# A twelve-sublayer network on one core: norm moments computed in the sublayer before, weight sums moved, and a skip term added in PSUM by a diagonal matrix

## The reference, cut to what matters

```python
def _layernorm(x, axis=-1, eps=1e-05):
    m = jnp.mean(x, axis=axis, keepdims=True)
    v = jnp.var(x, axis=axis, keepdims=True)
    return (x - m) / jnp.sqrt(v + eps)

x = x + sublayer(_layernorm(x, axis=-1), ...)       # twelve times, with twelve sublayers
```

```python
_, ys = jax.lax.scan(step, state0, xs)
y = jnp.moveaxis(ys, 0, -1)
y = y + D[None, :, None] * u
y = y * jax.nn.silu(z)
```

## Time and profile before

| | |
|---|---|
| runs | 2441.73, 2445.35, 2446.42 us, median 2445.35 |
| profiled execution | 2442.86 us |
| its span | 2441.0 us |
| mean granted clock of PE | 0.864 of full speed |
| norm blocks of stages 4, 6, 7, 8, 9, 10, 11 | one each |

### The profile page before, as it was taken

How to read it: one execution, slowest core, us unless ns; L and a number is a source line. 1 busy time by engine, 2 the same in 40 slices (tenths; PEclk the granted TensorE clock), 3 DMA queues, 4 the chain that set the end, 5 groups by cost and what they waited for, 6 DMA issues and landing times. The chain is left out here.

```text
span 2441.0 us, 34752 instructions
## 1 busy us (share of the span) xinstructions
PE 1988.1 (81%) x11321; PEld 1310.9 (54%) x11337; DVE 1754.3 (72%) x3900; ACT 1345.1 (55%) x2646; POOL 420.7 (17%) x585
## 2 busy tenths in 40 slices
PE   6999999987666666766877895597999999958978
PEld 4776767764333333543654353455766676733545
DVE  6878888777999998647785874674736373568734
ACT  5777777766989896254334365423323333352641
POOL 2333333322111110003532000201101010110000
PEclk8999999997877777786787798598999999976989
DMA  5000000002111102304202100150000000042010
GB/s 222 3 2 2 3 3 2 1 1 99 58 59 59 40 1 66 114 9 86 54 2 75 51 3 18 49 201 2 1 2 0 2 0 2 1 115 70 16 37 18
DMA packets 62030, 94.52 MB, mean 39 GB/s; under 512 B 9403, under 2 KB 48139, under 8 KB 59415
## 3 DMA queue, kind: packets, MB, share of 16 engines
q1 hardware_dynamic: 58604, 87.81, 11.4%
q0 software_dynamic: 1728, 4.22, 0.8%
q10 hardware_dynamic: 1536, 0.49, 0.1%
HBM read 80.53 MB, written 10.49 MB: 37 GB/s over the span
## 5 line engine op out<-in xcount | busy, mean ns | idle before, releaser
L1260 DVE SCALAR_TENSOR_TENSOR moe_acc<-moee_eo,moe_wsel,moe_acc 128x256 f32<-128x256 bf16 x512 | 226.0, 512 | 0.6
L867 DVE SCALAR_TENSOR_TENSOR l_acc<-l_px,l0w_chan,l_acc 128x253 f32<-128x253 f32 (+2 forms) x288 | 137.6, 478 | 80.6 <-POOL l_acc L835 80.1
L1192 ACT CAST moee_eo<-moee_po 128x512 bf16<-128x512 f32 x256 | 132.5, 596 | 38.5 <-PE moee_po L1165 33.8
L1165 PE MATMUL moee_po<-moee_db,moee_hb 96*128 96x256 bf16 (+1 forms) x768 | 126.9, 329 | 26.1 <-ACT moee_eo L1192 15.5
L1150 PE MATMUL moee_pu<-moe_xb,moee_wb 128*128 128x512 bf16 x192 | 73.1, 522 | 83.4 <-DVE moee_ub L1249 83.4
L1165 PEld LDWEIGHTS moee_po<-moee_db,moee_hb 96*128 96x128 bf16 (+1 forms) x768 | 87.6, 116 | 73.0 <-ACT moee_eo L1192 20.9
L1704 ACT ACTIVATE l3xa_ex<-l3xa_pS 128x512 f32<-128x512 f32 x128 | 74.2, 606 | 81.1 <-PE l3xa_pS L1617 76.7
L1704 ACT ACTIVATE l2a_ex<-l2a_pS 128x512 f32<-128x512 f32 x128 | 73.8, 606 | 76.7 <-PE l2a_pS L1617 72.2
L540 PE MATMUL l_pz<-xT,l0w_w_in 128*128 128x256 f32 x384 | 111.4, 414 | 2.5 <-DVE l_sz L915 2.5
L351 PE MATMUL ln_pt<-ident,xn 128*128 128x128 f32 x176 | 39.6, 418 | 85.9 <-DVE xn L277 85.9
L540 PE MATMUL l_px<-xT,l0w_w_in 128*128 128x256 f32 x384 | 103.5, 394 | 4.3 <-DVE l_acc L867 4.3
(11 more groups left out here) (614 smaller groups left out, 5508.3 us busy)
## 6 DMA issues: line engine op xcount, KB each, us to landing
moe_wf<-in_moe_up SPq DMA_DIRECT2D x48, 256.0 KB, 2.8
l3w_w_in<-in_l_w_in SPq DMA_DIRECT2D x1, 8224.0 KB, 25.9
m1b_bc<-bc_rows SPq DMA_DIRECT2D x16, 512.0 KB, 10.4
moe_df<-in_moe_down SPq DMA_DIRECT2D x48, 128.0 KB, 3.2
l_qs<-parts_q SPq DMA_DIRECT2D x36, 128.0 KB
l0w_w_in<-in_l_w_in SPq DMA_DIRECT2D x2, 1536.0 KB, 12.7
l0w_w_out<-in_l_w_out SPq DMA_DIRECT2D x1, 3072.0 KB
parts_q<-l_pieces SPq DMA_DIRECT2D x16, 192.0 KB, 2.3
```

The costliest lines, as they stand in the source:

```text
L867: nc.vector.scalar_tensor_tensor(out=a, in0=px[:, 0:S - (L0_CONV - 1 - c)], scalar=w, in1=a, op0=ALU.mult, op1=ALU.add).then_inc(tap_done, 1)
L1165: last = nc.tensor.matmul(po[:, t, :], hb[rows, j % H, t * P:(t + 1) * P], db[rows, j % H, :], start=(n == 0), stop=(n == len(parts) - 1))
L1192: nc.scalar.copy(eo[:, e % 2, 2 * q:2 * q + 2, :], po[:, 2 * q:2 * q + 2, :]).then_inc(o_read, 1)
L1260: last = nc.vector.scalar_tensor_tensor(out=acc[:, t, :], in0=eo[:, e % 2, t, :], scalar=wsel[:, t, e:e + 1], in1=acc[:, t, :], op0=ALU.mu ...
```

## The change

1. `moments_ahead` computes moments (bn_stats, one `link`, bn_aggr) in the block before the norm, into buffers that now live for the whole kernel. `normalize` gets `ahead`, the number of tiles whose moments are there: 6 in stages 4, 6, 7, 9, 10 and 11, 4 in stage 8. It then begins with `guess(0)`. Stages 0, 1, 2, 3 and 5 stay.
2. The calls stand in attend behind residual(0), (1) and (2); in ternary, a tile at a time; in quant_experts ahead of `unscale(7)`; in half_tokens, a tile at a time; in the l3e block ahead of the wait for the projection.
3. ACT's table for Ln and Exp is loaded at the end of attend, ternary and half_tokens instead of at the start of the norm.
4. `scale_and_sum`: units 0 to 7 stand one at each tile of half_tokens, units 8 to 15 in the l3s block, behind the decay rows. The matmuls of L3166 move behind the token projections and wait for the last unit.
5. The ones in rowsL and rowsR are written by POOL in the half_tokens block.
6. m1b: POOL makes two diagonal matrices of D in m1a. PE adds them times u into py, two matmuls a batch, where DVE's L2149 is removed; the gate multiplication reads py. The first of the two waits for `y_done` of the batch before.

```diff
+def moments_ahead(nc, g, link, tiles):
+    for t in tiles:
+        last = nc.vector.bn_stats(g["stats"][:, t, :], g["res"][:, t, :])
+    link(last)
+    for t in tiles:
+        nc.vector.bn_aggr(g["mv"][:, t, :], g["stats"][:, t, :])
...
+                if ahead:
+                    guess(0)
+                    for t in range(ahead, NT):
+                        stat(t)
+                    newton_a(0)
+                    for t in range(ahead, NT - 1):
+                        aggregate(t)
+                    newton_b(0)
+                    aggregate(NT - 1)
...
                 newton_c(0)
                 guess(1)
                 shifts(0)
...
-                nc.scalar.preload_act_table_set(EXP_LN)
+                if not ahead:
+                    nc.scalar.preload_act_table_set(EXP_LN)
...
# attend, DVE
-                        residual(batch_at(j, ADD_AT))
+                        u = batch_at(j, ADD_AT)
+                        residual(u)
+                        if u < B - 1:
+                            dve.wait_ge(added, u + 1)
+                            moments_ahead(nc, g, link, range(ST * u, ST * (u + 1)))
...
# m1a, POOL
+                    for n in range(M1_ET):
+                        nc.gpsimd.tensor_scalar(skip[:, n, :], g["ident"][:, :], chan[:, n, 6:7], None, ALU.mult)
...
# m1b, DVE
-                        for n in range(M1_ET):
-                            nc.vector.scalar_tensor_tensor(out=y[:, n, :], in0=u[:, n, b * S:(b + 1) * S],
-                                                           scalar=chan[:, n, 6:7], in1=py[:, n, :],
-                                                           op0=ALU.mult, op1=ALU.add).then_inc(read_done, 1)
-                        dve.wait_ge(read_done, M1_ET * (b + 1))
-                        nc.vector.tensor_tensor(y[:, :, :], y[:, :, :], res4(gate)[:, b, :, :],
+                        nc.vector.tensor_tensor(y[:, :, :], py[:, :, :], res4(gate)[:, b, :, :],
                                                 ALU.mult).then_inc(y_done, 1)
...
# m1b, PE
                     for i, (b, c, n) in enumerate(units):
+                        if b >= 1 and i % U == 0:
+                            pe.wait_ge(hc_done, i + 1)
+                            pe.wait_ge(y_done, b)
+                        if c == 0:
+                            nc.tensor.matmul(py[:, n, :], skip[:, n, :], u[:, n, b * S:(b + 1) * S], start=(n == 0),
+                                             stop=False)
                         pe.wait_ge(hc_done, i + 1)
                         if n == M1_ET - 1 and i + 1 < len(units):
                             spread_c(*units[i + 1][:2])
-                        if b >= 1 and i % U == 0:
-                            pe.wait_ge(read_done, M1_ET * b)
...
# ternary, DVE
+                        if 1 <= t < NT - 1:
+                            dve.wait_ge(summed, t)
+                            moments_ahead(nc, g, link, (t - 1,))
...
# half_tokens, POOL, then DVE
+                    for rows in ahead["rows"]:
+                        nc.gpsimd.memset(rows[:, :, :], 1.0)
...
-                    for j in range(L3_J // 2):
-                        scale_and_sum(dve, link, j)
                     dve.wait_ge(second_in, 32)
                     for t in range(NT):
-                        for j in range(L3_J // 2 + 2 * t, min(L3_J // 2 + 2 * t + 2, L3_J)):
-                            scale_and_sum(dve, link, j)
+                        if t == 0:
+                            dve.wait_ge(ahead["out_in"], 32)
+                        scale_and_sum(nc, link, ahead, t)
+                        if 1 <= t < NT - 1:
+                            dve.wait_ge(out_chain, t)
+                            moments_ahead(nc, g, link, (t - 1,))
                         dve.wait_ge(down, t + 1)
...
# quant_experts, DVE
                     unscale(6)
+                    dve.wait_ge(early_added, 2)
+                    moments_ahead(nc, g, link, range(0, 2 * ST))
                     unscale(7)
...
# mamba3_ends, DVE
+                    if start is None:
+                        moments_ahead(nc, g, link, range(NT - ST))
                     dve.wait_ge(used, ST)
...
                 if end is None:
+                    for j in range(NT, L3_J - 1):
+                        scale_and_sum(nc, link, m, j)
...
```

More of the change, by code:

```diff
@@ L2264, with scale_and_sum @@
 MOD_KEEP = S // 2
+def scale_and_sum(nc, link, m, j):
+    w_out, sums, gamma, beta = m["w_out"], m["sums"], m["chan"][:, j, 1:2], m["chan"][:, j, 2:3]
+    row = w_out[:, j, 0:D]
+    if j == 0:
+        nc.vector.memset(w_out[:, :, D:D + 1], 1.0)
+        link(nc.vector.tensor_scalar(sums[:, 1, :], row, beta, None, ALU.mult))
+        link(nc.vector.tensor_scalar(row, row, gamma, None, ALU.mult))
+        return
+    link(nc.vector.scalar_tensor_tensor(out=sums[:, 1, :], in0=row, scalar=beta, in1=sums[:, 1, :],
+                                        op0=ALU.mult, op1=ALU.add))
+    link(nc.vector.tensor_scalar(row, row, gamma, None, ALU.mult))
+    before = w_out[:, 0, 0:D] if j == 1 else sums[:, 0, :]
+    link(nc.vector.tensor_tensor(sums[:, 0, :], before, row, ALU.add))
 def half_tokens(nc, g, ahead):
@@ L2294, in half_tokens @@
             rope = g["xn"][:, :, :].rearrange("p (n t) d -> p n (t d)", n=2)
-            w_out, chan, sums = ahead["w_out"], ahead["chan"], ahead["sums"]
+            w_out, chan = ahead["w_out"], ahead["chan"]
             ph = st.psum("ph", [P, 4, 512])
@@ L3163, in _ @@
                                          start=True, stop=True).then_inc(used, 1)
-                if end is None:
-                    for n in range(2):
-                        last = nc.tensor.matmul(po[:, n, 0:D], g["ones"][:, 0:P], m["sums"][:, n, :], start=True,
-                                                stop=True)
-                    last.then_inc(gw_ready, 1)
                 if start is not None:
@@ L3178, in _ @@
                         last.then_inc(proj, 1)
+                if end is None:
+                    pe.wait_ge(sums_done, 1)
+                    for n in range(2):
+                        last = nc.tensor.matmul(po[:, n, 0:D], g["ones"][:, 0:P], m["sums"][:, n, :], start=True,
+                                                stop=True)
+                    last.then_inc(gw_ready, 1)
             @block.scalar
@@ L3376, in build @@
         g["ones"] = sbuf("ones", [P, S])
+        g["stats"] = sbuf("stats", [P, NT, 6])
+        g["mv"] = sbuf("mv", [P, NT, 2])
         g["ident"] = sbuf("ident", [P, P])
```

105 lines of the change are left out of this document (54 added, 51 removed).

## The result

The changed kernel took 2422.80 us, median of five runs (2417.99 to 2430.98), beside 2445.35 for the kernel before (2441.73 to 2446.63, five runs). The ratio is 0.9913, 95% interval 0.9891 to 0.9935. That is 22.5 us faster, where 15.0 was forecast. So the range was just wide enough, or just not. The profiled execution took 2422.80, the one of before 2442.86, so the two traces differ by 20.1, a little less than the medians.

The account below looks back on a forecast made before the run. No single engine was taken as the bound; each touched block was read for which wait ends last. Norms 16.2 plus half_tokens 7.6, less attention 6.3, m1b 2.3 and small ones 0.2, gave 15.0 us faster: 2430.3 us, range 2423 to 2439.

Parts of the forecast that it names:

- Norms: Norms of stages 4 and 6 to 11: moments made ahead and memsets moved shorten them by 16.2 us together.
- half_tokens: Down projection in half_tokens: PE no longer waits for DVE's weight units, eight tiles take 27.7 us, gain 7.6.
- Rival F: half_tokens: the weight move does nothing, as tile 0 waits for something else; 7.4 us faster, 2438; chance 0.02.
- l3s and the small ones: l3s costs 0, from −0.7 to +1; moments in the last mamba3 block, quant_experts and ternary cost 0.2 us together.
- so 2.1 each in stages 6 and 10; in stage 3 I take 1.8: Attention: moments cost 1.05 us a call at residuals 0 and 1; 6.3 in all with third residuals, ends 2 and 8.
- Rival B: Positional attention: PE idle of some 1.6 us brings two half-clock stretches costing 3.4 each; 8 us faster, 2437; chance 0.16.
- PEclk at 0.50 inside attention: Attention: PE granted half its clock there, given as a sign that the prediction is wrong and B or E holds.
- Rival E: All three attentions, residuals 0 and 1: six half-clock stretches cost 20.4 us; 5.4 slower, 2450.7; chance 0.04.
- Sum +2.3: m1b: three batch boundaries cost 1.2, 1.2 and 0.8 us, the end gains 0.9; +2.3 us, ends −2 and +6.
- over 5 of idle: m1b: sign in the profile after that hc of unit 2 comes with over 5 us of idle, 4.49 before.
- Rival C: Blocks behind norms: half-clock stretch keeps its length, losing 1.15 us per shortened norm; 9 us faster, 2436; chance 0.10.
- Rival D: Norms: transposes starting before the clock falls take about half of 3.7 us; 21 us faster, 2424; chance 0.06.

Follow-up runs that it names:

- e9: The changed kernel with attention's moments moved behind the last maximum and stage 11's second weights loaded last, waited for before its first down projection: 2406.53 us, ratio 0.9858.
- e5: The changed kernel with the scale_and_sum weight units back in their old places: 2428.70 us, ratio 0.9935 to the kernel before.
- e4: The changed kernel without moments in attention; norms of stages 4, 7 and 11 take all eight tiles: 2418.49 us, ratio 0.9899 to the kernel before.
- e6: The changed kernel with two more bn_stats per attention call, into a buffer nobody reads: 2428.99 us, ratio 0.9927 to the kernel before.
- e8_no_term: The changed kernel with m1b's skip term (D times u) left out entirely: 2429.79 us, ratio 0.9945 to the kernel before.
- e2: The changed kernel with attention's moments moved from the residuals to steps behind the last maximum: 2414.92 us, ratio 0.9877 to the kernel before.
- e3: The kernel before with only m1b's skip term moved to PE (in PSUM): 2437.98 us, ratio 0.9969 to the kernel before.

## Why the prediction was right, and where it was not

**The total: in part luck.** 15.0 was forecast and some 20 came between the traces, but not by the terms of the sum. m1b was 10.7 better than its term, ternary and the projections behind it 3.9, and half_tokens 1.3; attention was 6.3 worse, the norms 1.2, and the start of stage 3 lay 2.7 later by nothing in the change. That these cancel as far as the edge of the range is luck. What the prediction had right are the norms and half_tokens.

**Norms: right.** 16.2 forecast, 15.0 between the traces. Most of the missing 1.2 is stage 11, where the gain of 0.2 was a loss of 0.7 by a slower landing; the limit, the DMA, was named, and e9 shows it.

**half_tokens: right.** The down projection without gap was forecast at 27.7 and took 27.89 instead of 35.40, 7.5 less where 7.6 was forecast; e5 puts the worth of the move at 6.8. Rival F is dead: the gap returns with the units.

**l3s and the small ones: right**, −0.1 and within the spread.

**Attention: mechanism right, term too small.** The step that failed is "so 2.1 each in stages 6 and 10; in stage 3 I take 1.8". The 1.05 a call passes one for one, at 1.04 in stage 3 too, where 1.8 was too little for two calls. But the clock of rivals B and E comes on top: 8.7 in all for 6.3. Rival B was right about the place and the wait of 1.58, for residual 1 of stage 10 in that trace, and too dear in price. PEclk at 0.50 inside attention, which the prediction gave as a sign of being wrong, was there. The stretch was 3.4 us and not 6.8, and cost 2.46 − 1.05 = 1.4 and not 3.4 (from the maximum at residual 1 over two groups passed 12.45, and 9.99 in the kernel before). Rival E, all six, didn't come; stage 6 had no such stretch behind residuals 0 and 1 in any profile with the calls alone, stage 3 had some.

**m1b: wrong sign.** The step that failed is "Sum +2.3": it took both prices of the skip matmuls, at half and at full clock, and never asked what they do to the clock itself. Its work part is confirmed: 0.68 a boundary at full clock for 0.8. The "over 5 of idle" ahead of unit 2's product, given as a sign, was 2.79. I also counted VectorE's saved 1.2 a boundary only as an earlier start of PE, which at full clock is all it is. The profiles with the skip term on PE have m1b at 140.3 in the mean of eight, 7.4 under the two without it and without fillers; as three boundaries and the end sum to some +1 by work, 8 to 9 of gain are the clock's. It is the mechanism of rivals B and E with the sign turned: I allowed for PE's idle time to lower the clock in attention, and didn't allow for more PE work to raise it in m1b.

**Ternary and the projections of stage 6: not foreseen.** They got 3.8 shorter with no edit to their matmuls. In the traces with the skip term on VectorE ternary took 8.9 to 9.0, in seven of nine with it on PE 7.1, but 9.1 to 9.4 in e4 and e6. What differs is the clock. In the kernel before, PE's half-clock stretch around the norm of stage 5 is 13.7 us long and reaches 3.6 us into ternary; in the changed one it is 6.8 long and ends before it. The first group of the projections of stage 6, after:

```profile
1295.65 1.95 PE L1374 MATMUL l2p_pm<-xT,l_w 128*128 128x512 f32 x4 [1.26 <-PEq L72]
```

and in the kernel before:

```profile
1303.41 3.75 PE L1354 MATMUL l2p_pm<-xT,l_w 128*128 128x512 f32 x4 [1.26 <-PEq L72]
```

1.95 against 3.75, with the same matmuls. That m1b leaves this behind is likely for ternary, by the split above, though e4 and e6 don't keep to it. For the projections it isn't shown: they took the shorter time in five of the nine profiles with the skip term on PE and in e8_no_term, and the longer one in e2, e3, e4 and e6. So about half of the 3.8 is luck.

**Rival C** is refuted for this trace: no block behind a norm got longer by 1. Rival D, that transposes would start before the clock falls, wasn't seen: L371 takes 3.3 to 3.8 in every norm that was changed.

The gate product, with one input in PSUM, took 0.68 with POOL busy, not the 0.98 of the earlier trace rows with two SBUF inputs. That is the low end taken in the sum. Here the trace agrees with the Trainium skill ("SBUF — State Buffer", "Who interferes with whom"), which says that a VectorE instruction with at most one SBUF input doesn't contend with GpSimd, outside its two-port performance modes.

## What to carry to other kernels

Price an edit on PE's side of a boundary twice: by its work at the present clock, and by what it does to PE's idle time there. In m1b a boundary without fillers was followed by half clock (1.2 instead of 2.4 GHz) in 25 of 33 cases and one with them in none of 9, so an edit that adds matmuls can win by it, and one that removes them can lose 13 us. It is no certainty: a wait of 3.77 left the clock at 1.00, and one of 1.58 was followed by a stretch at half. Put extra work of a nearly full engine where the pipeline drains, and look first at what else ends a stage, here a DMA landing. A gain of a few us in a kernel whose clock moves needs the same block from several traces, and inside the block the steps that the edit touches: one m1b of 138.76 against 133.99 looked like a failure of the fillers, and wasn't.

## What the runs showed of the hardware

Removing work made m1b 15 us longer: 154.62 without any skip term, 139.38 with it on PE; 2.4 of this stand ahead of the first boundary. Six matmuls whose result nobody reads, 2.75 us a boundary, made it 13.7 shorter (147.67 to 133.99), nearly all of it behind the first of them. In another kernel with the same m1b code it was 138.76, by stretches at half clock that began where no fillers stood. Blocks that are the same in all kernels take different times: stage 3 starts at 951.1 to 957.1. A memset by POOL, which only writes SBUF, held a VectorE tensor_scalar of 4 columns for the whole 3.5 us (3.49 instead of 0.17), and the two bn_stats behind it ended together with it (3.41 instead of 0.75).
